# Strassen jobs beside the attention units, and the output projection as one Strassen block product

## The chip, the cores and the metric

One core of a Trainium2 chip. Its engines are TensorE (PE in the profile), VectorE (DVE), ScalarE (ACT), GpSimd (POOL) and SyncE (SP, which only issues transfers here). They run their own instruction streams and meet at semaphores. The metric is the device time of one execution in microseconds.

## The reference

A decoder layer on x of 2 x 512 x 1024 with a context of 2 x 1024 x 1024, in three parts that are each added to x:

```python
q, k, v = ln(x) @ Wq, ln(x) @ Wk, ln(x) @ Wv      # 32 query heads, 8 key/value heads of 128
q, k = rope(q), rope(k)
attn = softmax(causal(q @ k.T / sqrt(128)))       # 4 query heads share a key/value head
x = x + (attn @ v) @ Wo                           # Wo: 4096 x 1024
x = x + fake_quant(ln(x)) @ fake_quant(ctx)       # 8 bit grids
x = x + experts(ln(x))                            # top 16 of 64 low-rank experts
```

## The kernel before

Every float32 product is made of three passes on float32r pairs (`PASSES`): a high part that ScalarE casts (`*_high`) and a low part, the difference, that VectorE or GpSimd makes (`*_low`). TensorE does high by high, high by low, low by high.

**Projections.** `PANELS = 12` panels of 512 output features: K (0, 1), Q (2 to 9), V (10, 11). Each panel is one Strassen (Winograd) block product of the form [features x inner] by [inner x rows], with seven products P1 to P7 on halves; the blocks of x are made once (`fills`, in `xc`). Weight quarters A00, A10, A01, A11 arrive in `wraw`; GpSimd makes the sums S1, S3, S2, S4 in place of the quarters (`weight_sum`), and the low parts (`w_low`, L431). VectorE adds the products up and turns queries and keys (`rope`, L710 to L714). Results go to DRAM (`qk_dram`, `v_dram`).

**Attention units.** 64 units, one for each head and batch; unit u belongs to head group u // 8 and batch (u % 8) // 4. TensorE runs for unit u: `scores(u)` (L1001, 12 matmuls), a piece, `mix(u-1)` (L1029), a piece, `turn_probs(u)` (L1018, 10 transposes). Between, VectorE reads the scores with the mask (`peaks`, L792), ScalarE takes the exponentials (`exps`, L595), VectorE scales (`normalise`, L805), and after the transposes ScalarE and VectorE split the turned probabilities (`probs_high`, `probs_low`). Each query tile is loaded (ring of three), cast by ScalarE (`q_high`, L572) and split by GpSimd (`q_low`, L476) one unit ahead. `mix` is cast and split (`out_high`, `out_low`).

**Pieces.** The output projection is 128 pieces of 12 matmuls (`piece`, L1042) in banks 6 and 7, each of one group's four heads, 128 rows and 512 columns, and VectorE adds each to `resid` (`add_piece`, L821). Units 5 to 63 hold two each; nine come after the last mix. Wo is split by ScalarE and GpSimd in the units (`wo_high`, `wo_low`, L481), and the context is quantised there (`scale_ctx`, `quant_ctx`).

**The order** is written out by hand in every engine's program: five loops over u, with the position of each call fixed. x is loaded a second time into `resid` when the last panel is stored (L402), since the projections work in it. After the pieces VectorE takes the row statistics, and a second block of instructions (`mix_and_experts`, from L1131 on) begins when all engines have ended the first.

```python
for u in range(UNITS):            # TensorE
    scores(u)
    for n in pieces_of(u)[:1]: piece(n)
    if u > 0: mix(u - 1)
    for n in pieces_of(u)[1:]: piece(n)
    turn_probs(u)
```

## Time and profile before

| | us |
|---|---|
| median of three runs | 1380.82 (1379.29 to 1381.46) |
| the profiled execution | 1379.72 |
| its span | 1377.9 |
| TensorE busy in the span | 1319.8 (96%) |
| VectorE, ScalarE, GpSimd busy | 913.1, 610.7, 552.0 |

The span is what the trace covers. Its stages: blocks of x and first products to about 57 us, panels to 505, units from 505 to 1174, the last pieces to 1201, the second block from 1207 on. In a timeline a row gives start, duration, engine, line and operation; "x10" is a run of ten instructions; brackets hold the idle time before it and what ended it. The mean of a matmul counts its whole way through the array, so two overlap: the pitch of starts is what a matmul costs. PEclk is the granted share of TensorE's 2.4 GHz. Spans on POOL are rough.

### The profile page before, as it was taken

The numbers are of one execution on the slowest core, as the hardware profiler recorded it, in microseconds if no ns is written. First come the engines' busy times: TensorE is split into PE (matmuls) and PEld (weight loads), VectorE is DVE, ScalarE is ACT, GpSimd is POOL, SyncE is SP. The second block draws the span as 40 slices with busy tenths as digits, with TensorE's granted clock in tenths as the row PEclk, the third lists the DMA queues.
The fourth block names the chain that finished last, engine by engine and source line by source line (L and its number), as shares of the span: only waits on it lengthen the run. The fifth ranks groups of instructions, "written<-read, shape, count | busy, mean of one in ns | idle before, by whom it ended". The sixth has DMA issues, their size and how long they took to land. (4 is left out here: it accounts for less than half of the span.)

```text
span 1377.9 us, 19834 instructions
## 1 busy us (share of the span) xinstructions
PE 1319.8 (96%) x7217; PEld 1131.7 (82%) x7217; DVE 913.1 (66%) x2108; ACT 610.7 (44%) x1236; POOL 552.0 (40%) x290
## 2 busy tenths in 40 slices
PE   5999999999999986999999999999999999988998
PEld 4778888888889986888888888888888888766887
DVE  7788777777776235666666676576666666678653
ACT  3512222122222236566565565556656565156540
POOL 5676776666676643223142241323313232022000
PEclk9999999999999998999999999999999999999999
DMA  7033333232333156112223222222312210300001
GB/s 259 9 130 123 115 115 114 87 111 89 113 115 123 62 195 211 54 41 90 71 85 92 70 84 62 85 69 70 107 39 84 78 61 1 122 3 16 32 32 46
DMA packets 78432, 119.32 MB, mean 87 GB/s; under 512 B 5744, under 2 KB 42608, under 8 KB 78336
## 3 DMA queue, kind: packets, MB, share of 16 engines
q1 hardware_dynamic: 78336, 118.06, 26.0%
q8 instruction: 58, 0.95, 0.3%
q14 instruction: 38, 0.31, 0.1%
HBM read 88.68 MB, written 29.36 MB: 86 GB/s over the span
## 5 line engine op out<-in xcount | busy, mean ns | idle before, releaser
L977 PE MATMUL banks<-xc,wring 128*128 128x512 f32 x1680 | 385.5, 391 | 5.8 <-DVE banks L748 3.3
L977 PEld LDWEIGHTS banks<-xc,wring 128*128 128x128 f32 x1680 | 316.0, 189 | 72.7 <-issue 6.8
L476 POOL TENSOR_TENSOR q_lo<-q_raw,q_hi 128x512 fp32r<-128x512 f32 x64 | 83.0, 1297 | 452.8 <-ACT q_hi L572 452.8
L431 POOL TENSOR_TENSOR wring<-wraw,wring 128x1024 fp32r<-128x1024 f32 x72 | 172.7, 2399 | 120.2 <-ACT wring L553 120.2
L1042 PE MATMUL banks<-wo_hi,oT_hi 128*128 128x512 f32 x512 | 203.5, 398 | 2.5 <-DVE resid L821 2.5
L1042 PE MATMUL banks<-wo_hi,oT_lo 128*128 128x512 f32 x512 | 200.8, 392 | 0.0
L1042 PE MATMUL banks<-wo_lo,oT_hi 128*128 128x512 f32 x512 | 200.6, 392 | 0.0
L553 ACT CAST wring<-wraw 128x1024 fp32r<-128x1024 f32 x72 | 75.7, 1053 | 273.2 <-PE banks L977 116.3
L595 ACT ACTIVATE prob<-prob,shift 128x512 f32<-128x512 f32 (+3 forms) x256 | 140.9, 552 | 34.6 <-DVE shift L792 33.1
L588 ACT CAST pT_hi<-banks 128x512 fp32r<-128x512 f32 (+1 forms) x192 | 86.6, 524 | 149.6 <-PE banks L1018 149.6
L821 DVE TENSOR_TENSOR resid<-banks,resid 128x512 f32<-128x512 f32 x128 | 87.9, 687 | 88.6 <-PE banks L1042 88.4
L783 DVE TENSOR_TENSOR pT_lo<-banks,pT_hi 128x512 fp32r<-128x512 f32 (+1 forms) x192 | 103.8, 595 | 24.9 <-ACT pT_hi L588 24.9
L1042 PEld LDWEIGHTS banks<-wo_hi,oT_lo 128*128 128x128 f32 x512 | 96.1, 188 | 20.9
L1042 PEld LDWEIGHTS banks<-wo_hi,oT_hi 128*128 128x128 f32 x512 | 96.4, 188 | 19.5 <-issue 2.9
L792 DVE CUSTOM_DVE_ANT_0 prob<-banks,mask 128x512 f32<-128x512 f32 (+3 forms) x256 | 110.1, 485 | 1.3 <-PE banks L1001 0.8
L1042 PEld LDWEIGHTS banks<-wo_lo,oT_hi 128*128 128x128 f32 x512 | 96.4, 188 | 16.3
L1018 PE MATMUL banks<-ident,prob 128*128 128x128 f32 x640 | 82.7, 277 | 16.9 <-DVE oT_lo L810 12.9
L1018 PEld LDWEIGHTS banks<-ident,prob 128*128 128x128 f32 x640 | 74.7, 143 | 26.8 <-DVE prob L805 16.6
L1001 PE MATMUL banks<-kT_hi,q_hi 128*128 128x512 f32 (+3 forms) x256 | 89.3, 349 | 0.0
L1001 PE MATMUL banks<-kT_lo,q_hi 128*128 128x512 f32 (+3 forms) x256 | 84.4, 330 | 0.0
L1001 PE MATMUL banks<-kT_hi,q_lo 128*128 128x512 f32 (+3 forms) x256 | 84.1, 328 | 0.0
L1029 PE MATMUL banks<-pT_hi,v_lo 128*128 128x512 f32 (+3 forms) x256 | 82.8, 323 | 0.0
(169 smaller groups left out, 2369.1 us busy)
## 6 DMA issues: line engine op xcount, KB each, us to landing
qk_dram<-resid SPq DMA_DIRECT2D x80, 256.0 KB, 2.0
wraw<-in_L_attn_Wq SPq DMA_DIRECT2D x32, 512.0 KB, 4.5
q_raw<-qk_dram SPq DMA_DIRECT2D x64, 256.0 KB, 4.0
raw<-in_L_attn_Wo SPq DMA_DIRECT2D x32, 512.0 KB, 4.1
resid<-in_x SPq DMA_DIRECT2D x16, 512.0 KB, 8.0
spare<-in_ctx SPq DMA_DIRECT2D x16, 512.0 KB, 3.7
wraw<-in_L_attn_Wk SPq DMA_DIRECT2D x8, 512.0 KB, 9.5
wraw<-in_L_attn_Wv SPq DMA_DIRECT2D x8, 512.0 KB, 4.4
```

What stands on the lines that cost most here:

```text
L431: nc.gpsimd.tensor_tensor(wring[:, 1, n % 3, :], factor(s, p), as32(wring[:, 0, n % 3, :]), ALU.subtract).then_inc(w_lo, 1)
L476: nc.gpsimd.tensor_tensor(qh[1][:, u % 3, :], q_raw[:, u % 3, :], as32(qh[0][:, u % 3, :]), ALU.subtract).then_inc(q_lo, 1)
L588: nc.scalar.copy(pT[0][:, CHUNKS[c][0]:CHUNKS[c][0] + CHUNK_WIDTH[c]], turned_chunk(turned, mixed, c)).then_inc(pT_hi, 1)
L595: nc.scalar.activation(prob[:, sl], prob[:, sl], ACT.Exp, bias=shift[:, i:i + 1], scale=-1.0, accum_out=total[:, i:i + 1]).then_inc(exp_do ...
L783: nc.vector.tensor_tensor(pT[1][:, sl], turned_chunk(turned, mixed, c), as32(pT[0][:, sl]), ALU.subtract).then_inc(pT_lo, 1)
L792: nc.vector.tensor_tensor_reduce(out=prob[:, PROB_AT[i]:PROB_AT[i] + w], in0=score[:, s, c:c + w], in1=mask[:, H - w:H], scale=-SCALE, sca ...
L821: nc.vector.tensor_tensor(resid[:, t, sl], bank[n % 2][:], resid[:, t, sl], ALU.add).then_inc(added, 1)
L977: ins = nc.tensor.matmul(dst, wring[:, a, n % 3, k * 256 + fb * P:k * 256 + (fb + 1) * P], xc[:, XI[p], c, k, :], start=first, stop=(k == ...
L1001: ins = nc.tensor.matmul(score[:, s, c:c + w], qh[a][:, u % 3, i * P:(i + 1) * P], kT[e][:, h % 2, 0:w], start=(p == 0), stop=(p == 2))
L1018: ins = nc.tensor.transpose(dst[:, col:col + P], prob[:, PROB_AT[i] + j * P:PROB_AT[i] + (j + 1) * P], ident[:])
L1029: ins = nc.tensor.matmul(mixed[:, j * P:H], vv[a][:, h % 2, j, :], pT[c][:, KEYS_AT[j]:KEYS_AT[j] + w], start=(j == 0 and p == 0), stop=(j ...
L1042: ins = nc.tensor.matmul(bank[n % 2], oT[a][:, h % 2, k, t * P:(t + 1) * P], wo[c][:, 2 * half + k // 2, (k % 2) * 512:(k % 2) * 512 + 512 ...
```

## The change

**Projections.** `PANELS` is 5: K (0, 1), the queries of head group 0 (2), V (3, 4). The queries of groups 1 to 7 are 14 narrow panels (`NARROW`) of 256 features, each again a Strassen product of seven; each of its products is one job of 12 matmuls of 512 columns (`job`), 98 in all. `PLACES` puts them in the units: one in unit 1, two in each of units 2 to 33, then two or one, to unit 52, at the places where the pieces were. The order within a narrow panel is `SEQ`. Weights come as four loads of 256 KB for a panel (`load_narrow`), ScalarE casts them (`narrow_high`), GpSimd makes sums and low parts (`narrow_sums`, `narrow_low`), VectorE reads the banks and multiplies by the rope tables (`read_job`), GpSimd adds the two halves (`turn_added`), SyncE stores (`keep_turned`). The last panel's P5 and P3 partly move into units 0 and 1. The rings of queries go from three to two.

**Output projection.** The heads' outputs are stored to DRAM by name (`keep_out`, batch 1 with the sign turned, by `O_STORES` up to four copies of 256 KB a unit), and GpSimd adds blocks of four heads onto the copies with accumulating DRAM to DRAM transfers (`accumulate`, 28 of 1 MB), which gives the sums S1 to S4. The product is then one Strassen product over batch, half of the heads and half of the columns. P1 is in 16 first steps of 12 matmuls (`first_step`, 15 of them in units 56 to 63, with `first_high` and `first_low`). The other six products (`OUT`) are 8 steps of 24 matmuls each (`step`), after the last unit; `step_high` and `step_low` split both operands, `wt` makes Wo's differences on VectorE, `read_banks` and `add_copies` add to `resid`. The second load of x, the quantising of the context, and the load of A_w and B_w move to this stage. Wo's quarters are loaded whole as the memory of the jobs comes free, half of the last one (`w01_b`) after the last mix.

```diff
-PANELS = 12
+PANELS, TURNED = 5, 3
+LASTP = PANELS - 1
...
+SEQ = ("P1", "P6", "P2", "P7", "P5", "P4", "P3")
+NARROW = 14
+JOBS = 7 * NARROW
+PLACES = ([(1, 1)] + [(u, p) for u in range(2, 34) for p in (0, 1)]
+          + [(u, p) for u in range(34, UNITS) for p in (0, 1) if p == 0 or u % 4 != 1])
+JOB_AT = {pl: j for j, pl in enumerate(PLACES[:JOBS])}
...
+OUT = ("P2", "P3", "P6", "P7", "P5", "P4")
+PAIRS = 8
+FIRST_STEPS = 2 * PAIRS
+REST = [(u, p) for u in range(LAST_JOB_UNIT + 2, UNITS) for p in (0, 1)]
+STEP_AT = {pl: n for n, pl in enumerate(REST[len(REST) - FIRST_STEPS + 1:])}
...
         def load_q(u):
-            if u >= 3:
-                sp.wait_ge(q_lo, u - 2)
-            sp.dma_start(q_raw[:, u % 3, :], qk_dram[GROUPS + 4 * (u // 8) + u % 4, (u % 8) // 4]
-                         ).then_inc(q_in[u % 3], 16)
...
+                sp.wait_ge(q_lo, u - 1)
+            if u >= 8:
+                n = turn_needed(u)
+                sp.wait_ge(q_kept[n % 2], 16 * (n // 2 + 1))
...
+        def keep_out(u):
+            sp.wait_ge(o_copied, u + 1)
+            for name in o_names(u):
+                sp.dma_start(o_dram[name][o_place(u)[1]], o_st[u % 2][:]).then_inc(o_kept[u % 2], 16)
...
+        def load_step(s):
+            m, q = s // PAIRS, s % PAIRS
+            if s < 2:
+                sp.wait_ge(fa_lo, FIRST_STEPS - 1 + s)
+            else:
+                sp.wait_ge(oa_lo, s - 1)
+            name = {"P2": "A01", "P3": "S4", "P6": "S2", "P7": "S3", "P5": "S1", "P4": "N11"}[OUT[m]]
...
+            if (s, c) == (LASTP, "C10"):
+                sp.wait_ge(w_lo, len(ORDER))
+                load_narrow(0)
+                load_narrow(1)
+        for u in range(1, UNITS):
+            if u + 2 < UNITS:
+                load_q(u + 2)
+            if u % 4 == 1 and half_of(u) + 1 < HALVES:
+                load_kv(half_of(u) + 1)
+            if (u - 1, 0) in JOB_AT:
...
+                keep_turned(JOB_AT[u - 1, 0])
+            if u >= 2:
+                keep_out(u - 2)
+            for j in jobs_of(u):
+                if j % 7 == 6 and j // 7 + 2 < NARROW:
+                    load_narrow(j // 7 + 2)
+            if (u - 1, 1) in JOB_AT:
+                keep_turned(JOB_AT[u - 1, 1])
...
+        keep_out(UNITS - 2)
+        load_first(FIRST_STEPS - 1)
+        load_step(0)
+        load_step(1)
+        keep_out(UNITS - 1)
+        sp.wait_ge(mix_done, UNITS)
+        load_wo(w01[1], PAIRS, 1, w01_in[1])
         for t in range(TT):
             sp.dma_start(resid[:, t, :], x_t[t]).then_inc(x_in[t], 16)
...
+        load_ctx(0)
+        load_ctx(1)
+        for s in range(2, STEPS):
+            load_step(s)
+            n = s - 4 * PAIRS
+            if 2 <= n < 2 * KT:
+                load_ctx(n)
+            if s == 4 * PAIRS:
+                sp.wait_ge(wt_sum, 4 * PAIRS)
+                sp.dma_start(a_rows[:], A_w.rearrange("(n p) c -> p n c", p=P)).then_inc(rows_in, 16)
+                sp.dma_start(b_rows[:], B_w.rearrange("(n p) c -> p n c", p=P)).then_inc(rows_in, 16)
...
+        def narrow_low(j):
+            pool.wait_ge(n_hi, j + 1)
+            nc.gpsimd.tensor_tensor(n_ring(1, j), n_factor(j), as32(n_ring(0, j)), ALU.subtract).then_inc(n_lo, 1)
...
+        def narrow_sums(j):
+            e, use = j // 7, 16 * (j // 14 + 1)
+            if j % 7 == 1:
+                pool.wait_ge(n_in[e % 2][QUARTER["A10"]], use)
+                pool.wait_ge(n_in[e % 2][QUARTER["A11"]], use)
+                nc.gpsimd.tensor_tensor(n_ta[:], n_quarter(e, "A10"), n_quarter(e, "A11"), ALU.add).then_inc(n_sum, 1)
+                nc.gpsimd.tensor_tensor(n_quarter(e, "A10"), n_quarter(e, "A00"), n_quarter(e, "A10"),
+                                        ALU.subtract).then_inc(n_sum, 1)
+                pool.wait_ge(n_sum, 4 * e + SUMS["S3"])
+                nc.gpsimd.tensor_tensor(n_quarter(e, "A00"), n_ta[:], n_quarter(e, "A00"),
+                                        ALU.subtract).then_inc(n_sum, 1)
+            elif j % 7 == 6:
+                pool.wait_ge(n_in[e % 2][QUARTER["A01"]], use)
+                pool.wait_ge(n_sum, 4 * e + SUMS["S2"])
+                nc.gpsimd.tensor_tensor(n_quarter(e, "A01"), n_quarter(e, "A01"), n_quarter(e, "A00"),
+                                        ALU.subtract).then_inc(n_sum, 1)
...
+        def turn_added(j):
+            if SEQ[j % 7] not in TURNS:
+                return
+            n = 4 * (j // 7) + TURNS[SEQ[j % 7]]
+            pool.wait_ge(job_read, 6 * (j // 7) + j % 7)
...
+            nc.gpsimd.tensor_tensor(q_made[:, n % 2, :], n_turn[:, 0, :], n_turn[:, 1, :], ALU.add
+                                    ).then_inc(turn_made, 1)
+        def accumulate(name, source, g, before):
+            k = 4 * (g % 4)
+            if before:
+                pool.wait_ge(s_added[name], 16 * before)
+            nc.gpsimd.dma_start(out=o_dram[name][k:k + 4].rearrange("k p c -> (k p) c"),
+                                in_=o_dram[source][k:k + 4].rearrange("k p c -> (k p) c"),
+                                accum_op=ALU.add, max_dma_last_dim=8192).then_inc(s_added[name], 16)
...
         for u in range(UNITS):
+            if (u - 1, 0) in JOB_AT:
+                turn_added(JOB_AT[u - 1, 0])
             if u >= 1 and u + 1 < UNITS:
                 q_low(u + 1)
             if u % 4 == 2 and half_of(u) + 1 < HALVES:
                 k_low(half_of(u) + 1)
                 v_low(half_of(u) + 1)
-            for m in wo_after(u):
-                wo_low(m)
+            for j in jobs_of(u + 1):
+                narrow_sums(j)
+                narrow_low(j)
+            if (u - 1, 1) in JOB_AT:
+                turn_added(JOB_AT[u - 1, 1])
+            for f in steps_of(u + 1):
+                first_low(f)
+            if u % 8 == 2 and u >= 8:
+                accumulate_negated(u // 8 - 1)
+            if u % 8 == 6 and u >= 32:
+                accumulate_plain(u // 8)
+        first_low(FIRST_STEPS - 1)
+        accumulate_negated(GROUPS - 1)
...
+        def narrow_high(j):
+            e, p = j // 7, SEQ[j % 7]
...
+            if p in ("P1", "P2", "P4"):
+                act.wait_ge(n_in[e % 2][QUARTER[FACTOR[p]]], 16 * (e // 2 + 1))
+            else:
+                act.wait_ge(n_sum, 4 * e + SUMS[{"P6": "S2", "P7": "S3", "P5": "S1", "P3": "S4"}[p]])
+            nc.scalar.copy(n_ring(0, j), n_factor(j)).then_inc(n_hi, 1)
...
         for u in range(UNITS):
             if u > 0:
                 probs_high(u - 1)
+                if (u - 1, 1) in JOB_AT:
+                    keep_job(JOB_AT[u - 1, 1])
+                if (u - 1, 1) in STEP_AT:
+                    keep_first(STEP_AT[u - 1, 1])
                 if u + 1 < UNITS:
                     q_high(u + 1)
             if u % 4 == 2 and half_of(u) + 1 < HALVES:
                 k_high(half_of(u) + 1)
                 v_high(half_of(u) + 1)
-            for m in wo_after(u):
-                wo_high(m)
+            for j in jobs_of(u + 1):
+                narrow_high(j)
+            if (u + 1, 0) in STEP_AT:
+                first_high(STEP_AT[u + 1, 0])
             exps(u)
             normalise_wide(u)
+            if (u, 0) in JOB_AT:
+                keep_job(JOB_AT[u, 0])
+            if (u, 0) in STEP_AT:
+                keep_first(STEP_AT[u, 0])
+            if (u + 1, 1) in STEP_AT:
+                first_high(STEP_AT[u + 1, 1])
             if u > 0:
-                out_high(u - 1)
-            if u % 4 == 1:
-                scale_ctx(half_of(u))
+                keep_out(u - 1)
         probs_high(UNITS - 1)
-        out_high(UNITS - 1)
+        first_high(FIRST_STEPS - 1)
+        step_high(0)
+        keep_out(UNITS - 1)
+        keep_first(FIRST_STEPS - 1)
+        for s in range(1, STEPS):
+            step_high(s)
...
+        def read_job(j):
+            e, p, b = j // 7, SEQ[j % 7], job_bank(j)
+            if p == "P1":
+                return
...
+                dve.wait_ge(job_read, 6 * e + 3)
+                nc.vector.tensor_tensor(n_u[:, 0, :], b, n_u[:, 0, :], ALU.add)
+                link(nc.vector.tensor_tensor(b, b, n_u[:, 1, :], ALU.add))
+                job_turn(b, 4 * e + TURNS[p])
+            elif p == "P4":
...
+        def step_low(s):
+            m, q = s // PAIRS, s % PAIRS
+            dve.wait_ge(oa_hi, s + 1)
+            nc.vector.tensor_tensor(oa[1][:, s % 2, :, :], oraw[:, s % 2, :, :], as32(oa[0][:, s % 2, :, :]),
+                                    ALU.subtract).then_inc(oa_lo, 1)
+            dve.wait_ge(ob_hi, s + 1)
+            nc.vector.tensor_tensor(ob[1][:, s % 2, :, :], out_factor(m, q), as32(ob[0][:, s % 2, :, :]),
+                                    ALU.subtract).then_inc(ob_lo, 1)
...
+        def read_banks(m):
+            p = OUT[m]
+            dve.wait_ge(step_done, PAIRS * (m + 1))
...
+        for s in range(STEPS):
+            m, q = s // PAIRS, s % PAIRS
+            step_low(s)
+            if m < 4:
+                wt(m, q)
+            else:
+                quant_ctx(s - 4 * PAIRS)
+            if m >= 1 and q == 1:
+                read_banks(m - 1)
+            if m >= 1 and q == 2:
+                add_copies(m - 1)
+            if m == 5 and 3 <= q < 3 + TPB:
+                row_stats(nc, resid, stats, moments, q - 3, link)
+        row_scale_in(nc, moments, lnw, slice(0, TPB), var_ready)
+        quant_rows(0)
+        read_banks(5)
+        add_copies(5)
+        for t in range(TPB, TT):
             row_stats(nc, resid, stats, moments, t, link)
-        row_scale_in(nc, moments, lnw, slice(0, TPB), var_ready)
-        add_piece(PIECES - 8)
-        add_piece(PIECES - 7)
-        quant_rows(0)
-        for n in range(PIECES - 6, PIECES):
-            add_piece(n)
-            if n >= PIECES - 4:
-                dve.wait_ge(added, n + 1)
-                row_stats(nc, resid, stats, moments, n - (PIECES - 4) + TPB, link)
         row_scale_in(nc, moments, lnw, slice(TPB, TT), var_ready)
...
+        def job(j):
+            e, i, p = j // 7, j % 7, SEQ[j % 7]
+            pe.wait_ge(n_lo, j + 1)
...
+            for k in range(KH):
+                for n, (a, c) in enumerate(PASSES):
+                    ins = nc.tensor.matmul(job_bank(j), n_ring(a, j)[:, k * P:(k + 1) * P], xc[:, XI[p], c, k, :],
+                                           start=(opens and k == 0 and n == 0), stop=(k == KH - 1 and n == 2),
+                                           skip_group_check=True)
+            ins.then_inc(job_done, 1)
...
+        def step(s):
+            m, q = s // PAIRS, s % PAIRS
+            pe.wait_ge(oa_lo, s + 1)
+            pe.wait_ge(ob_lo, s + 1)
...
+            for k in range(2):
+                for t in range(TPB):
+                    for i, (a, c) in enumerate(PASSES):
+                        ins = nc.tensor.matmul(step_bank(m, t), oa[a][:, s % 2, k, t * P:(t + 1) * P],
+                                               ob[c][:, s % 2, k, :], start=(q == 0 and k == 0 and i == 0),
+                                               stop=(q == PAIRS - 1 and k == 1 and i == 2), skip_group_check=True)
+            ins.then_inc(step_done, 1)
...
             scores(u)
-            for n in pieces_of(u)[:1]:
-                piece(n)
+            if u == 0:
+                product(LASTP, "P5", (1,))
+                product(LASTP, "P3", (0,))
+            if u == 1:
+                product(LASTP, "P3", (1,))
+            place(u, 0)
             if u > 0:
                 mix(u - 1)
-            for n in pieces_of(u)[1:]:
-                piece(n)
+            place(u, 1)
             turn_probs(u)
-        piece(PIECES - 10)
+        first_step(FIRST_STEPS - 1)
         mix(UNITS - 1)
-        for n in range(PIECES - 9, PIECES):
-            piece(n)
-        pe.wait_ge(masked_done, 4 * UNITS)
+        for s in range(STEPS):
+            step(s)
```

## Rows read from the trace of the kernel before

**Rows 1.** Table of stretches, 700 to 800 us; the header names the columns.
```profile
core 0: us, PE busy (x) PEld busy (x) DVE busy (x) ACT busy (x) POOL busy (x), PEclk, DMA share, GB/s
700.00:800.00 100.00, 99.84 (x552) 86.91 (x551) 64.41 (x188) 60.49 (x147) 30.99 (x20) 1.00 0.27 83
```

**Rows 2.** Timeline of GpSimd: start, us, line, operation; sums of two query panels.
```profile
379.34 2.40 POOL L439 TENSOR_TENSOR ta<-wraw 128x1024 f32<-128x1024 f32 x1
...
417.47 2.41 POOL L439 TENSOR_TENSOR ta<-wraw 128x1024 f32<-128x1024 f32 x1
```

**Rows 3.** Timeline of TensorE over one unit.
```profile
706.65 1.25 PE L1018 MATMUL banks<-ident,prob 128*128 128x128 f32 x10
707.66 0.48 PE L1001 MATMUL banks<-kT_hi,q_hi 128*128 128x512 f32 x1
...
709.67 0.40 PE L1042 MATMUL banks<-wo_hi,oT_hi 128*128 128x512 f32 x1
...
712.44 0.39 PE L1029 MATMUL banks<-pT_hi,v_hi 128*128 128x512 f32 x1
...
714.30 0.45 PE L1042 MATMUL banks<-wo_hi,oT_hi 128*128 128x512 f32 x1
...
717.11 1.25 PE L1018 MATMUL banks<-ident,prob 128*128 128x128 f32 x10
```

**Rows 4.** Timeline of ScalarE over the same unit.
```profile
708.51 0.65 ACT L572 CAST q_hi<-q_raw 128x512 fp32r<-128x512 f32 x1
...
710.16 0.73 ACT L595 ACTIVATE prob<-prob,shift 128x512 f32<-128x512 f32 x1
```

**Rows 5.** Timeline of GpSimd in the same unit.
```profile
709.23 1.30 POOL L476 TENSOR_TENSOR q_lo<-q_raw,q_hi 128x512 fp32r<-128x512 f32 x1 [6.78 <-ACT q_hi L572]
```

**Rows 6.** Timeline of VectorE in the same unit.
```profile
712.71 0.88 DVE L805 TENSOR_SCALAR prob<-prob,inv 128x384 f32<-128x384 f32 x3
```

**Rows 7.** Waits of TensorE: waited for, us in total, times, longest.
```profile
PE banks L1018 <- DVE oT_lo L810: 12.9, 10, 5.8
PE banks L1018 <- DVE prob L805: 4.0, 1, 4.0
...
PE banks L1042 <- DVE resid L821: 2.5, 1, 2.5
```

**Rows 8.** Table of stretches in the first units.
```profile
511.40:515.90 4.50, 4.46 (x22) 4.22 (x23) 2.46 (x6) 3.04 (x6) 1.00 (x1) 0.65 0.95 349
521.00:526.50 5.50, 5.50 (x27) 5.06 (x25) 4.01 (x12) 2.62 (x6) 1.60 (x2) 0.69 1.06 378
532.40:540.30 7.90, 7.86 (x34) 7.31 (x34) 4.12 (x14) 5.83 (x14) 3.63 (x2) 0.62 0.45 160
549.50:552.00 2.50, 2.44 (x18) 2.35 (x18) 1.16 (x2) 1.78 (x4) 0.00 (x0) 1.00 0.00 0
```

**Rows 9.** Groups by line: line, operation, busy us, mean ns, idle before.
```profile
L710 DVE TENSOR_TENSOR resid<-banks,sin 64x512 f32<-64x512 f32 x80 | 55.4, 693 | 3.6 <-PE banks L977 1.3
```

**Rows 10.** DMA issues of the page: count, KB, median us to landing.
```profile
q_raw<-qk_dram SPq DMA_DIRECT2D x64, 256.0 KB, 4.0
```

**Rows 11.** Timeline of TensorE, two units without a piece.
```profile
541.77 1.28 PE L1018 MATMUL banks<-ident,prob 128*128 128x128 f32 x10 [1.49 <-DVE oT_lo L810]
...
549.56 1.28 PE L1018 MATMUL banks<-ident,prob 128*128 128x128 f32 x10 [2.62 <-DVE oT_lo L810]
```

**Rows 12.** DMA view of 506 to 527 us.
```profile
DMA packets 3058, 7.07 MB, mean 337 GB/s; under 512 B 247, under 2 KB 1027, under 8 KB 3056
```

**Rows 13.** Timeline of ScalarE in that stretch.
```profile
523.90 0.62 ACT L572 CAST q_hi<-q_raw 128x512 fp32r<-128x512 f32 x1 [1.92 <-DMA q_raw<-qk_dram]
```

**Rows 14.** Timeline at the end of attention, VectorE.
```profile
1201.48 0.69 DVE L821 TENSOR_TENSOR resid<-banks,resid 128x512 f32<-128x512 f32 x1 [0.46 <-PE banks L1042]
...
1203.77 0.17 DVE L168 TENSOR_SCALAR lnw<-moments 128x4 f32<-128x4 f32 x1
...
1206.88 0.69 DVE L1351 TENSOR_SCALAR raw<-raw 128x1024 f32<-128x1024 f32 x1 [0.96 <-PEq L116]
```

More of the change, by code:

```diff
@@ L124, in build @@
[L124 to L126 removed]
+            with ExitStack() as sems:
+                attention(nc, hold(sems), sems, x_t, Wq, Wk, Wv, Wo, cos_in, sin_in, (x1s, x1z, x2s, x2z),
+                          ctx_in.rearrange("b k n -> (b k) n"), qk_dram, v_dram, o_dram, A_w, B_w, proj, heads,
+                          narrow, outp, *shared)
             mix_and_experts(nc, hold(es), es, out_t, Wr, keys, *shared)
```

674 lines of the change are left out of this document (464 added, 210 removed).

## The prediction

> **What bounds the kernel now.** I read the table of stretches first, then a timeline of one attention unit on each engine, then the waits, and the chain of waits last, which covers only the final stages. In a stretch of attention TensorE is busy 99.8 of 100 us at a granted clock of 1.00 (2.4 GHz), VectorE 64, ScalarE 60, GpSimd 31 [rows 1]: TensorE sets the time. The panels of projections are as full: one panel of queries takes 38.13 us for 168 matmuls of 512 columns, 0.227 us each [rows 2]. A unit takes 10.46 us: transposes 1.01, scores 2.01, a piece 2.77, mix 1.86, a piece 2.81 [rows 3]. That is 4.88 of attention and 2.79 for each of two fillers of 12 matmuls.
>
> Inside that period the other engines run one chain. Counted from the start of the transposes (706.65), ScalarE ends the high part of the next queries at 2.5 and starts the exponentials at 3.5 [rows 4]; GpSimd ends the low part of those queries at 3.9 [rows 5]; VectorE ends the last scaled probabilities at 6.9, which is 3.4 after the exponentials began [rows 6]. TensorE asks for them at 10.46. So the exponentials may begin 3.5 us late before TensorE waits. That slack is what the change lives on.
>
> **What the matmuls give.** Projections have the same matmuls before and after: 5 panels, and 98 jobs of 12 in place of 7 panels of 168. The output projection had 128 pieces of 12 (1536); it gets 16 first steps of 12 and 48 steps of 24 (1344). 192 fewer x 0.227 = **-43.6 us**, all on TensorE. The waits of TensorE in the first units (12.9 + 4.0) and for one piece bank after the last unit (2.5) go too, since the units 1 to 4 get fillers: **-19.4** [rows 7]. With them goes slow clock: 4.5 x 0.35 + 5.5 x 0.31 + 7.9 x 0.38 = **-6.3** [rows 8]. By this alone the span would be 1377.9 - 69.3 = 1308.6.
>
> **What the jobs add beside the units.** VectorE gets 18 operations for 7 jobs at 0.7 us [rows 9] instead of three for a unit, 3.6 us a unit against 2.1: busy about 79%, behind exponentials and matmuls, costed at nothing (without that cover 1.5 us a unit, 80 us). SyncE issues up to 13 transfers in a unit, and the query load has a ring of two in place of three; I cost it at nothing while a load takes the 4.0 us of the median [rows 10], and return to it as a rival.
>
> The cost that I do see is an order. In iteration u ScalarE runs `narrow_high` for the jobs of u+1 before `exps(u)`. For P6 it waits for S2, the third of three sums that GpSimd makes in `narrow_sums` of the same iteration, behind `q_low(u+1)`, which itself waits for ScalarE. Queued behind the waiting ScalarE instruction are the exponentials, and TensorE's transposes wait for those. A 512-column operation of GpSimd takes 1.30 [rows 5].
> - P6 in the second place: 3.9 (queries) + 1.3 (low of P1) + 3.9 (sums) = 9.1; high part 0.6; exponentials at 9.7, probabilities at 13.1 instead of 10.46: 2.7 us of wait.
> - P6 in the first place: the unit before had S4 ahead of P3, so its exponentials start at about 6.2, its probabilities end at 9.6, and VectorE's five operations of P5 end at 13.2, which is 2.8 in the new unit. `turn_added` 1.3, queries 1.3, sums 3.9 = 9.3; two high parts 1.2; + 3.4 = 14.0: 3.5 us of wait, or 2.9 where one place follows.
>
> `PLACES` puts P6 second in units 5, 12, 19, 26, 33 (5 x 2.7 = 13.5), first in 9, 16, 23, 30 (14.0) and in 37, 41, 45, 49 (4 x 2.9 = 11.6). Where keys and values are split in the same iteration GpSimd has 2.6 more: P6 of 19 and 23 (5.2), and P3 of units 11 and 15 (2.6 and 1.9). Together **+49**. A wait of 2.6 is followed by a clock of 1.00 here, one of 4.0 by 0.65 [rows 7, 8, 11]; so only the two longest pay for the clock, 1.5 each: **+3**. Its bounds are 0 and 15 x 3.0, the loss of the longest slow stretch.
>
> The start: the first weights are loaded after the last P4's tile, job 1 needs three sums, and query 2 is loaded behind 2 MB. Between 0 and 5.8 + 3.0 (the worst of the old start [rows 7, 8]), taken at **+2.8**. Units 53 to 55 have no filler: a unit without one took 549.56 - 541.77 = 7.8 [rows 11], less the removed VectorE step 7.1, against 4.88 of work: 3 x 2.2 = **+6.6**.
>
> **What the block product adds.** The last first step waits for high and low parts that start only after the last probabilities are copied, at 1.9 where now the query's cast begins [rows 4]: 0.6 on ScalarE, then GpSimd's 1.3 for 512 elements and about twice that for 1024, to 6.3, where TensorE is free at 1.0. **+5.3**, and 2 of clock. A step is 24 x 0.227 = 5.45 us; ScalarE needs at most four times 0.65 [rows 4] for it, 2.6, VectorE two subtractions and a weight difference of about 1.2 each (an estimate: 0.69 for 512 elements plus as much again less the start), 3.7. So steps are bound by TensorE, except where P5's four bank reads, the quantising of the context and the statistics meet: **+3**.
>
> The **restart** is the second large cost. After the last mix SyncE queues half of a Wo quarter (2 MB), all of x (4 MB), two context tiles (1 MB), and only then the load for step 2. The trace has this burst: 7.07 MB took 21 us at 337 GB/s, and a query load issued in it held ScalarE up [rows 12, 13]. 7.75 MB take 23 us; 11.8 + 23 = 34.3 after the last transposes, + 3.4 for high and low = 37.7, where steps 0 and 1 end at 21.8: 16 us. The last three accumulating transfers (3 MB, read twice and written once) run at the same time on the same engines. No row shows such a transfer; at nothing they leave 16, at twice their bytes and this rate they make it 33. I take **+20**, nearer the lower end since the row of 337 GB/s already had other traffic, and 3 for the clock. The Trainium skill ("DMA: Bandwidth & Descriptors", Anatomy of one DMA) gives a GpSimd-issued transfer about 2.0 us plus its bytes at 436 GB/s; by it, as an estimate, three of 1 MB would add some 7 us and this term would be 23. No run so far shows it.
>
> Loading A_w and B_w (4 MB) ahead of step 33's load delays it past its slack by **+4.3** (4.5 MB at 337 GB/s are 13.4 us, slack about 9). The tail: now 5.4 us lie between VectorE's read of the last piece and the next block, of which 1.6 are one tile's statistics and 3.1 the scales [rows 14]. Then it will be two bank reads and two additions of 1024 elements (5.1), four tiles' statistics (6.4) and 3.1, together 14.6: **+9.2**, and 1.4 for a clock that has fallen.
>
> **The sum.** 1308.6 + 2.8 + 49 + 3 + 6.6 + 7.3 + 23 + 3 + 4.3 + 10.6 = 1418.2 us of span. The profiled execution took 1379.72 with a span of 1377.9, so 1.8 more: **1420 us**. It was 1.1 below the median of 1380.82, which I leave aside.
>
> **Rivals.**
> - *The sums are not late* (faster). If GpSimd had S2 before ScalarE asks, the 49 + 3 vanish: 1368. For it: GpSimd is idle two thirds of the time [rows 1]. Against: it must run `q_low` first, which waits for ScalarE until 2.5.
> - *The restart is hidden as well*: also without the 23: 1345. For it: nothing but that the loads of steps 0 and 1 are ahead.
> - *Transfers are late in the units* (slower still). Stores of the signed sums (1 MB in a unit), weights (1 MB) and 3 MB of accumulation meet once per group of heads, and a late query load stops the exponentials as it did at 523.9. At 5.8 of wait + 3.0 of clock seven times: +62, 1482. It decides from a load of over about 8 us instead of 4; before, seen only in the burst.
> - The forecast itself is slower; the mechanism on the faster side decides at 3.5 us of lateness.
>
> **How the numbers follow.** Forecast 0.50; sums not late 0.16; restart hidden too 0.12; late transfers 0.12; in between, with part of the 49, 0.10, of which 0.05 lie below the old time, 0.04 at it and 0.01 above. The change does what it says in every case, since the counts follow from the loops. Faster by over 0.2% (about what a measurement can tell from no change): 0.16 + 0.12 + 0.05 = 0.33; within it 0.04; slower 0.50 + 0.12 + 0.01 = 0.63. The range reaches from the second rival to 30 above the forecast, which takes in the bounds of the restart and half of the clock's: 1348 to 1452. The forecast's own range is 1395 to 1450.
>
> **What would show it.** In the changed profile: ScalarE waiting for GpSimd's sum before `n_ring` of P6, some 13 times, and TensorE before the transposes in the same units, 2.5 to 3.5 us each (5 to 6 in two); a jobs unit without P6 still at 10.5; one gap of 15 to 33 us before the third step; steps of 5.45 us; about 14.5 us from the last step to the next block. No waits of ScalarE for GpSimd would make the first rival right; waits for `q_raw` the third. Wrong from the start would be a step bound by VectorE: at 6 us a step the product would cost 26 more.

## The result and the profile after

The changed kernel takes **1514.34 us** (median of 4 runs, 1510.90 to 1518.62), the kernel before 1381.11 beside it (1379.29 to 1381.46): a ratio of 1.0969, 95% interval 1.0939 to 1.0999. The forecast was 1420 with a range of 1348 to 1452. The direction was right, the size was not: the change costs 133 us, not 39.

The head of the page of the kernel after, with its two lines in 40 slices that moved most:

```profile
span 1508.9 us, 19933 instructions
PE 1302.0 (86%) x7025; PEld 1111.5 (74%) x7025; DVE 947.6 (63%) x2024; ACT 698.9 (46%) x1385; POOL 638.3 (42%) x451
...
PE   5999999998998898999999628682899989968998
...
PEclk9999999999999999999999869987899999999999
...
q0 software_dynamic: 4032, 29.36, 9.9%
```

TensorE was busy 96% of the span before. Now it is 86%, with the loss at slices 23 to 28, some 830 to 1060 us: the end of the attention units and the restart. The last line is a queue that the kernel before hardly used: 29.36 MB of accumulating transfers.

What ended the waits of the kernel after (engine, line waited at, releaser: us in total, times, longest):

```profile
PE banks L1457 <- DVE prob L1175: 51.7, 20, 7.6
ACT nring_hi_a L860 <- POOL nraw L697: 50.9, 8, 7.5
...
PE banks L1457 <- ACT o_st L925: 47.2, 12, 27.4
...
PE banks L1529 <- DVE ob_lo L1184: 39.6, 4, 31.4
ACT oa_hi L892 <- DMA oraw<-o_A: 35.3, 1, 35.3
ACT q_hi L846 <- DMA q_raw<-qk_dram: 34.4, 4, 25.1
ACT nring_hi_b L860 <- POOL nraw L697: 32.2, 5, 6.7
...
PE banks L1487 <- DVE n_turn L1113: 11.2, 17, 1.0
```

L1457 are the transposes of a unit, L1529 the 48 steps, L1487 the jobs. Against 19.4 us before [rows 7], TensorE now waits 98.9 before transposes and 39.6 before steps.

The table lays the forecast's sum beside TensorE's timeline, cut at the transposes of three units, at the last step's last matmul (row at 1323.49) and at the next block's first row (1337.57):

| stretch | forecast | after | difference |
|---|---|---|---|
| start to unit 1 | 251.2 | 251.4 | +0.2 |
| unit 1 to 51 (jobs) | 563.8 | 577.4 | +13.6 |
| unit 51 to 63 | 109.9 | 175.9 | **+66.0** |
| unit 63 to the last step (last first step, restart, 48 steps) | 306.3 | 318.8 | +12.5 |
| tail | 16.0 | 14.1 | -1.9 |
| rest | 171.0 | 171.3 | +0.3 |

The sum is 90.7 us. Nearly three quarters of it lie in twelve units, for which the sum had 6.6 us beyond their work. Below, a period is the time from one unit's transposes to the next unit's. TensorE's timeline there (start, us, line, operation, idle time before it and its releaser):

```profile
853.15 2.37 PE L1457 MATMUL banks<-ident,prob 128*128 128x128 f32 x10 [7.63 <-DVE prob L1175]
...
893.73 2.37 PE L1457 MATMUL banks<-ident,prob 128*128 128x128 f32 x10 [27.43 <-ACT o_st L925]
...
918.50 1.28 PE L1457 MATMUL banks<-ident,prob 128*128 128x128 f32 x10 [2.30 <-ACT o_st L925]
...
1010.96 0.77 PE L1503 MATMUL banks<-ob_hi,oa_hi 128*128 128x512 f32 x1 [5.04 <-POOL ob_lo L748]
1060.88 0.77 PE L1529 MATMUL banks<-ob_hi,oa_hi 128*128 128x512 f32 x1 [31.41 <-DVE ob_lo L1184]
```

The releaser named at 893.73 is only the last of a row. ScalarE's and SyncE's timelines show what stood ahead of it:

```profile
888.21 0.62 ACT L846 CAST q_hi<-q_raw 128x512 fp32r<-128x512 f32 x1 [25.05 <-DMA q_raw<-qk_dram]
```

```profile
851.75 18.65 SPq L499 DMA_DIRECT2D w<-in_L_attn_Wo  x8
870.44 5.62 SPq L499 DMA_DIRECT2D w_a<-in_L_attn_Wo  x2
876.16 2.60 SPq L467 DMA_DIRECT2D q_raw<-qk_dram  x1
```

SyncE issues ten transfers of 1 MB of output weights in unit 53, and only then the next query load. The DMA view of 838 to 895 us says how long that is:

```profile
DMA packets 9874, 18.71 MB, mean 328 GB/s; under 512 B 472, under 2 KB 1540, under 8 KB 9743
```

The long periods behind it (11.9 to 19.3 us in units 56 to 62, where the forecast has 10.46) have another cause, an order on ScalarE:

```profile
916.29 0.62 ACT L875 CAST oa_hi<-oraw 128x512 fp32r<-128x512 f32 x1 [0.26 <-PE banks L1503]
916.82 1.04 ACT L877 CAST ob_hi<-w 128x1024 fp32r<-128x1024 f32 x1
917.76 0.59 ACT L925 ACTIVATE o_st<-banks 128x512 f32<-128x512 f32 x1
```

The high copies of a first step wait until the step just done has left its ring place (first row), and the copy of the unit's output stands behind them. That copy frees the bank into which TensorE transposes at 918.50.

Part of the time is clock. In the stretch of those twelve units the granted clock is 0.85 (columns as in [rows 1]):

```profile
829.00:1005.00 176.00, 116.55 (x604) 101.45 (x603) 64.45 (x203) 89.10 (x203) 81.13 (x53) 0.85 0.61 190
```

### The profile page after: what moved, and what is told of

Its sections match the earlier page's. It is cut to its first block and busy times, and to the rows that moved or that the text cites. A ratio compares the mean times of both kernels' runs of the same rounds, so it can differ in the third digit from the quotient of the medians.

```text
span 1508.9 us, 19933 instructions
## 1 busy us (share of the span) xinstructions
PE 1302.0 (86%) x7025; PEld 1111.5 (74%) x7025; DVE 947.6 (63%) x2024; ACT 698.9 (46%) x1385; POOL 638.3 (42%) x451
## 3 DMA queue, kind: packets, MB, share of 16 engines
q0 software_dynamic: 4032, 29.36, 9.9%
## 5 line engine op out<-in xcount | busy, mean ns | idle before, releaser
L1529 PE MATMUL banks<-ob_hi,oa_hi 128*128 128x512 f32 x384 | 151.3, 394 | 39.6 <-DVE ob_lo L1184 39.6
L1457 PE MATMUL banks<-ident,prob 128*128 128x128 f32 x640 | 90.1, 293 | 99.1 <-DVE prob L1175 51.7
L1457 PEld LDWEIGHTS banks<-ident,prob 128*128 128x128 f32 x640 | 77.6, 150 | 115.1 <-DVE prob L1175 63.7
L1529 PE MATMUL banks<-ob_lo,oa_hi 128*128 128x512 f32 x384 | 150.8, 393 | 0.0
L1529 PE MATMUL banks<-ob_hi,oa_lo 128*128 128x512 f32 x384 | 150.6, 392 | 0.0
L913 ACT ACTIVATE prob<-prob,small 128x512 f32<-128x512 f32 (+3 forms) x256 | 140.8, 553 | 11.8 <-DVE small L1162 11.7
L1487 PE MATMUL banks<-xc,nring_hi_a 128*128 128x512 f32 x400 | 125.2, 394 | 5.0 <-DVE n_turn L1113 5.0
L1487 PE MATMUL banks<-xc,nring_hi_b 128*128 128x512 f32 x384 | 120.6, 395 | 6.2 <-DVE n_turn L1113 6.2
L1418 PE MATMUL banks<-xc,wring 128*128 128x512 f32 x504 | 119.2, 397 | 5.7 <-DVE banks L1085 3.3
L1418 PEld LDWEIGHTS banks<-xc,wring 128*128 128x128 f32 x504 | 95.8, 192 | 26.5 <-issue 6.7
L1529 PEld LDWEIGHTS banks<-ob_hi,oa_hi 128*128 128x128 f32 x384 | 73.1, 190 | 56.4 <-issue 41.2
L636 POOL TENSOR_TENSOR wring<-wraw,wring 128x1024 fp32r<-128x1024 f32 x30 | 71.9, 2399 | 58.6 <-ACT wring L827 58.6
## 6 DMA issues: line engine op xcount, KB each, us to landing
o_S<-o_S POOLq DMA_DIRECT2D x12, 1024.0 KB, 14.1
w<-in_L_attn_Wo SPq DMA_DIRECT2D x12, 1024.0 KB, 17.8
```

Of the source, the lines that this page charges most:

```text
L636: nc.gpsimd.tensor_tensor(wring[:, 1, n % 3, :], factor(s, p), as32(wring[:, 0, n % 3, :]), ALU.subtract).then_inc(w_lo, 1)
L913: nc.scalar.activation(prob[:, sl], prob[:, sl], ACT.Exp, bias=shift[:, i:i + 1], scale=-1.0, accum_out=total[:, i:i + 1]).then_inc(exp_do ...
L1418: ins = nc.tensor.matmul(dst, wring[:, a, n % 3, k * 256 + fb * P:k * 256 + (fb + 1) * P], xc[:, XI[p], c, k, :], start=first, stop=(k == ...
L1457: ins = nc.tensor.transpose(dst[:, col:col + P], prob[:, PROB_AT[i] + j * P:PROB_AT[i] + (j + 1) * P], ident[:])
L1487: ins = nc.tensor.matmul(job_bank(j), n_ring(a, j)[:, k * P:(k + 1) * P], xc[:, XI[p], c, k, :], start=(opens and k == 0 and n == 0), stop ...
L1529: ins = nc.tensor.matmul(step_bank(m, t), oa[a][:, s % 2, k, t * P:(t + 1) * P], ob[c][:, s % 2, k, :], start=(q == 0 and k == 0 and i == ...
```

## The experiments

All are measured beside the kernel before; differences are between medians. The theory is that the 133 us are independent losses (counted from the old kernel; from the sum's 1308.6 of matmuls, with the 1.8 outside the span, they are 204): GpSimd's sums (A), the weights ahead of the query loads (B), the order of the output's copy (C), the restart (D). The first four kernels undo one each.

**A: GpSimd's sums earlier.** `narrow_sums` makes P6's first two sums as part 0, its third as part 1 and P3's as part 2.

```diff
+        narrow_sums(0, 0)
         for u in range(UNITS):
...
             for j in jobs_of(u + 1):
-                narrow_sums(j)
                 narrow_low(j)
+                if j % 7 == 0:
+                    narrow_sums(j, 1)
+                elif j % 7 == 2:
+                    narrow_sums(j, 2)
+                elif j % 7 == 6 and j + 1 < JOBS:
+                    narrow_sums(j + 1, 0)
```

> Only the order of GpSimd's weight sums in the narrow jobs is changed: the two first sums of P6 follow the low copy of the previous column's last job, the third follows the low copy of P1, that of P3 follows the low copy of P2. Theory A (the exponentials of a unit stand on ScalarE behind a high copy that waits for these sums): the 14 long periods of 12.3 to 16.8 us fall to 10.5 to 11, GpSimd's sums no longer end a wait of ScalarE's ring copies, and the time falls from 1514 by 45 to 62 us, to 1452 to 1469. Rival: GpSimd is simply late in these units (key and value copies, the additions of the turned queries), so that the order of its work moves the wait to another place; then the time falls by less than 20 us, to above 1494.

1471.47 us (1470.76 to 1473.65): **42.9 us less**, 2 short of the range. ScalarE's waits for `nraw` fall from 127.7 us in 27 waits to these 21.5 in 5, and TensorE's wait for the probabilities falls with them:

```profile
ACT nring_hi_a L871 <- POOL nraw L701: 12.1, 3, 5.0
ACT nring_hi_b L871 <- POOL nraw L701: 9.4, 2, 5.9
...
PE banks L1468 <- DVE prob L1186: 20.7, 10, 8.6
```

The last was 51.7 in 20 waits. The mechanism holds, its size a little less than expected. What stays are units with a late chain of their own: in units 11 and 18 (periods of 13.0 and 13.2) ScalarE still waits 5.9 and 5.0 us for the third sum, which GpSimd reaches late behind the splits of keys and values (in unit 11 three accumulates to issue as well), and in unit 28 (13.2) the output's copy waits 6.1 us until its buffer has been stored.

**B: the weights in pieces**, each behind the unit's query load.

```diff
-                load_wo(w00, 0, 0, w00_in)
...
-                load_wo(w10, 2 * PAIRS, 0, w10_in)
-                load_wo(w11, 2 * PAIRS, 1, w11_in)
-                load_wo(w01[0], 0, 1, w01_in[0])
+            for n in WO_AT.get(u, ()):
+                load_piece(n)
```

> Only the issue of the output weights' first 14 MB on SyncE's queue is changed: one piece of 1 MB in each of units 51 to 62, two in 53 and 54, each behind the query load of its unit, instead of 4 MB in unit 51 and 10 MB in unit 53. Theory B (the query loads queue behind the weights, 18.71 MB at 328 GB/s): the periods of units 53 and 55 fall from 14.3 and 32.6 to about 11, ScalarE's waits of 7.8 and 25.1 us for q_raw go, and the time falls by 33 to 40 us, to 1474 to 1481. Rival (the loads would be as late through the transfers of the units themselves, stores and accumulates): a fall of less than 12 us, to above 1502, with the waits for q_raw moved to units 56 to 62.

1490.81 (1489.48 to 1495.34): **23.5 less**, not 33 to 40. Of the 34.4 us of waits for `q_raw` 1.1 are left, but 8.6 us before unit 55's transposes stay and unit 60 has become longer (period 23.1). ScalarE's timeline names another transfer in both places:

```profile
865.65 0.62 ACT L888 CAST oa_hi<-oraw 128x512 fp32r<-128x512 f32 x1 [5.15 <-DMA oraw<-o_A]
...
930.64 0.62 ACT L888 CAST oa_hi<-oraw 128x512 fp32r<-128x512 f32 x1 [8.01 <-DMA oraw<-o_A]
```

The second waits beside an accumulate. The DMA view of 918 to 944 us, 40 slices:

```profile
DMA  9999999999999996999999624910000000000000
GB/s 214 217 232 228 232 219 228 228 222 230 230 216 230 217 192 207 381 373 402 399 406 406 246 85 145 331 44 0 0 0 0 0 0 0 0 0 0 0 0 2
```

For ten microseconds all 16 engines are busy and move 220 GB/s; then the accumulates end and the same engines move 400. That is a fifth loss (E), which I had not separated.

**C: the output's copy first.**

```diff
+            if u > 0:
+                keep_out(u - 1)
             if (u + 1, 1) in STEP_AT:
                 first_high(STEP_AT[u + 1, 1])
-            if u > 0:
-                keep_out(u - 1)
```

> Only the order of two things on ScalarE is changed: the copy of the unit's output (o_st) goes ahead of the high copies of the first step of the next unit's second place. Theory C (the transposes of a unit wait for the copy of the output, which stands behind a copy that waits for the step just done): the waits of TensorE for the o_st copy in units 56 to 62, 47 us in 12 waits now, fall to below 12, and the time falls by 14 to 20 us, to 1494 to 1500; the three longest waits, with the accumulates about them, may stay. Rival: the output's copy is late for its own sake (the mix and the store of o_st two units earlier, slowed by the accumulates), so the wait stays over 35 us and the time within 5 us of 1514.

1500.64 (1497.48 to 1504.37): **13.7 less**. The ordinary first-step unit falls from 12.9 to 11.1 us and no wait for `o_st` is left among the large ones; the 26 us of unit 55 are put down to `prob` instead, which is the same query load by another releaser. The mechanism holds and the size is just short of its 14 to 20, with units 58 and 60 still long (15.3 and 17.9).

**D: the restart**, with what steps 2 to 11 don't need behind their loads.

```diff
-        load_wo(w01[1], PAIRS, 1, w01_in[1])
-        for t in range(TT):
-            sp.dma_start(resid[:, t, :], x_t[t]).then_inc(x_in[t], 16)
-        load_ctx(0)
-        load_ctx(1)
         for s in range(2, STEPS):
             load_step(s)
...
+            if 4 <= s < 4 + TT:
+                sp.dma_start(resid[:, s - 4, :], x_t[s - 4]).then_inc(x_in[s - 4], 16)
...
```

> Only SyncE's order after the last unit is changed: the last 2 MB of the output weights go in two pieces behind the loads of steps 2 and 3, the eight residual tiles behind the loads of steps 4 to 11, the first two context tiles behind that of step 14. Theory D1 (step 2's load stands in the queue behind 8 MB): the idle time before step 2 falls from 31.4 to 3 to 8 us and the time by 23 to 28 us, to 1486 to 1491. Theory D2 (the accumulates of the last group hold the DMA engines in that stretch): the idle time stays at 15 to 20 us and the time falls by 11 to 16 us, to 1498 to 1503.

1493.76 (1492.70 to 1495.33): **20.6 less**, where D1 had 23 to 28 and D2 11 to 16. The idle time of 31.41 before step 2 is gone; what TensorE still waits there is 2.95 before step 3 and 4.09 before step 4:

```profile
1040.45 0.77 PE L1536 MATMUL banks<-ob_hi,oa_hi 128*128 128x512 f32 x1 [2.95 <-DVE ob_lo L1191]
...
1053.05 0.55 PE L1536 MATMUL banks<-ob_hi,oa_hi 128*128 128x512 f32 x1 [4.09 <-DVE ob_lo L1191]
```

So D1 names what step 2 waited for, and part of it came back behind: TensorE's waits before steps are 15.3 in all, from 39.6.

**Together, and without the accumulates.**

> The four edits (sums earlier, weights in pieces, order of the output's copy, order after the last unit) together. Each alone took from 1514.3: 42.8, 23.5, 13.7 and 20.5 us, in all 100.5. If they are independent losses, as the theory has it, the time is 1414 (1408 to 1420). If they share a cause (one wait uncovers another), the sum is not reached and the time stays above 1425.

1420.56 (1416.88 to 1422.63), **93.8 less** where the four alone add up to 100.7. They are nearly independent, though the time is 0.6 above the expected range. That this is the number forecast is chance; it says only how much was overlooked.

> The changed kernel without any of its 28 accumulating transfers (the combinations of the attention outputs are not added up in memory, so the output is another). Theory E (these transfers, while they run, hold all DMA engines at some 220 GB/s where 400 go otherwise, and so lengthen the first-step units and the restart): the idle time before step 2 falls from 31.4 to 18 to 22 us, the long periods of units 59 to 61 fall to the 12.9 of their neighbours, 9 us in all, nothing changes before unit 52, and the time falls by 18 to 24 us, to 1490 to 1496. Rival (the accumulates only run in time that nobody needs): within 5 us of 1514.

1477.77 (1476.20 to 1482.24): **36.6 less**, half as much again as theory E allowed. By the timeline 17.8 of it lie between units 51 and 63 and 15.4 in the restart, where the idle time is

```profile
1026.73 0.76 PE L1525 MATMUL banks<-ob_hi,oa_hi 128*128 128x512 f32 x1 [16.01 <-DVE ob_lo L1180]
```

Theory E had the wrong units: 13.2 of the 17.8 us lie in units 53 to 55, where an accumulate meets the burst of weights (their periods fall from 14.3, 8.0 and 32.6 to 8.4, 7.1 and 26.2). Units 59 to 61, where E expected 9 us, fall by 2.9 in all, and unit 60 still takes 18.1.

The DMA views of the two restarts, first the kernel after (1014 to 1060), then without accumulates (997 to 1027):

```profile
GB/s 0 0 0 0 0 235 212 360 378 399 390 281 201 239 265 224 285 217 278 224 292 224 289 203 281 228 310 406 417 431 417 413 427 399 408 388 387 157 7 0
...
q0 software_dynamic: 432, 3.15, 32.8%
...
o_S<-o_N POOLq DMA_DIRECT2D x3, 1024.0 KB, 17.7
```

```profile
GB/s 0 0 0 0 0 112 251 175 344 377 410 380 412 407 423 407 393 426 404 393 426 426 382 421 426 393 404 426 393 410 421 385 388 388 390 142 0 0 0 60
```

Three accumulates of 1 MB took 32.8% of 46 us on all engines, 15.1 us, or 209 GB/s. That is about the 15.4 us by which the idle time differs.

> The four edits, and none of the 28 accumulating transfers (the output is another). It prices these transfers where the four losses are gone. Theory E: the first-step units fall to periods of about 10.5 to 11, the restart's idle time to under 3 us, and the time is 1385 to 1395, some 20 to 28 us below the four edits. Rival: the loads in pieces are what collides with the query loads, with or without the accumulates: less than 8 us below the four edits.

1386.01 (1385.29 to 1386.76), 34.6 below the four edits: more than expected, and about the price that the accumulates have beside the other losses. No idle time is left before steps 2 to 4, but units 58 and 60 stay at 15.3 and 16.0, so their length isn't the accumulates' either.

**The accumulates of the last group moved**, alone in the changed kernel:

```diff
-        accumulate_negated(GROUPS - 1)
+        one_negated(GROUPS - 1, 0)
+        pool.wait_ge(step_done, 10)
+        one_negated(GROUPS - 1, 1)
+        pool.wait_ge(step_done, 18)
+        one_negated(GROUPS - 1, 2)
```

> The changed kernel with one edit: of the last group's three accumulates only that into S4, which the second product reads, follows the last unit; that into S2 waits for step 10 and that into S1 for step 18. Without all accumulates the idle time before step 2 was 16.0 instead of 31.4 us. Theory G (the restart pays for the bytes of the accumulates that run in it): with one of the three left it is 20 to 23 us, and the time falls by 8 to 11 us, to 1503 to 1506. Rival (the plain accumulate of unit 62 and the first one already fill the stretch in which step 2's load waits): below 4 us.

1502.32 (1499.91 to 1502.72): **12.0 less**, one more than expected, and the idle time before step 2 is 21.53. With three accumulates in the restart it is 31.4, with one 21.5, with none 16.0: about 5 us for each.

**The search for a version that gains.** Five more kernels and one of them without accumulates build on the four edits; their edits are told in the expectations.

> The four edits, with each unit's weight piece behind the first-step loads instead of ahead of them, and three more: the adapters' weights in eight pieces from step 34 on instead of two transfers ahead of step 33's load; the copies of P1 added to the last quarter of the rows during P7's successor, and half of the last four tiles' statistics taken ahead of the last read; the three accumulates of groups 5 and 6 one a unit instead of three in a row. Expected against the four edits: 8 us from the adapters' weights (waits of 8.2 us in the step stage), 5 from the tail (2.49 of additions and 4 x 0.69 of statistics), 5 to 10 from the first-step units: 1390 to 1397. Rival: the VectorE's own time in the last steps is the limit, and the tail keeps its length.

1398.38 (1397.53 to 1400.36), 22.2 below the four edits and 1 above the expected range. The wait of 7.2 us for the adapters' weights is gone, and the tail's last wait is `PEq` 3.6 where it was 8.5.

> The eight edits of the run before, and three in the attention units: ScalarE's and GpSimd's work on the next half's values goes one unit behind that on its keys; the last first step's high copies go ahead of the last unit's probabilities (and its load ahead of a store); the copies of the first eight first steps' banks go ahead of unit 60's exponentials. Expected from the trace of the run before: 5 us from the last first step (idle 6.2 before it), 3 to 5 from unit 60 (period 15.97), 4 from unit 58 (period 15.28, idle 4.66), 3 to 6 from the long periods of units 11 to 28: 1398 less 15 to 20, 1378 to 1384, level with the kernel before. Rival: ScalarE is full in these units whatever the order (the work is only handed to the next unit), and the time stays above 1390.

1383.73 (1383.27 to 1387.40), 14.7 less again; ratio to before 1.0029 (1.0017 to 1.0041). ScalarE was late by its order, not full: unit 60 falls to 12.0 and unit 58 to 11.2.

> As the run beside it, but the accumulating transfers take each head's output from SBUF (112 of 256 KB, three or one for a head, issued by GpSimd in every unit) instead of 28 of 1 MB from memory to memory; the data read again from memory fall by 29 MB. Theory F1 (an accumulating transfer costs DMA time by the bytes that it adds, wherever these come from): the same time as the run beside it within 4 us, with the transfers spread over the units but two of the last ones still in the restart. Theory F2 (the reading back is a third of the load): 4 to 10 us faster. Rival: 84 more issues of some 0.85 us on GpSimd make its low copies late: over 5 us slower.

1398.03 (1397.10 to 1399.22): 14.3 **slower** than the run beside it. The rival is right in its sign alone. TensorE waits 33.4 us in 12 waits for the output's copy, and ScalarE makes that copy late because the buffer is still being read:

```profile
ACT o_st L951 <- DMA o_S<-o_st: 34.3, 15, 5.8
```

```profile
833.36 2.62 POOL L757 DMA_DIRECT2D o_S<-o_st  x3
...
844.21 0.60 ACT L951 ACTIVATE o_st<-banks 128x512 f32<-128x512 f32 x1 [5.81 <-DMA o_S<-o_st]
```

So the delay comes from the held buffer and not from low copies. GpSimd's order has a part in it: unit 53's copy was made at 818.14, its three additions were issued at 833.36 only, and unit 55's copy could start when they had landed. How much is the late issue and how much the transfer, no run separates. F1 and F2 both fail, since the DMA time of the same bytes has grown. The lines of that queue, first of e_eleven (span 1381.9), then of e_direct (span 1395.3):

```profile
q0 software_dynamic: 4032, 29.36, 10.9%
```

```profile
q0 software_dynamic: 16128, 29.37, 13.4%
```

151 us against 187, for four times as many packets. (The transfers also run at other times than those of e_eleven, so the 14.3 are not all due to the source.)

> The eleven edits and two more: the first 4 MB of the output weights in units 51 and 52, two pieces each, so that units 53 and 54 carry one piece of the next instead of two; and VectorE's sums on the last 2 MB of the output weights in steps 6 and 7 instead of 4 to 7. The trace of the eleven edits has ScalarE waiting 7.45 us for q_raw in unit 55 (TensorE idle 7.42) and TensorE idle 2.02 and 7.03 before steps 4 and 5. If both go: 1383.7 less 12 to 16, 1368 to 1372, faster than the kernel before by 0.6 to 0.9 %. Rival: the plain accumulate of unit 54 (at 230 GB/s for 10 us) makes the query load late whatever stands ahead of it, and the last accumulates do so in the restart: above 1379.

1383.06 (1381.51 to 1385.51): no gain; its rival is right. The idle time moved to units 54 and 57 (5.4, and a period of 12.8) and stayed in the restart. There ScalarE waits for step loads issued beside three accumulates:

```profile
944.50 1.05 ACT L937 CAST oa_hi<-oraw 128x1024 fp32r<-128x1024 f32 x1 [7.79 <-DMA oraw<-o_A]
...
956.54 1.04 ACT L937 CAST oa_hi<-oraw 128x1024 fp32r<-128x1024 f32 x1 [10.04 <-DMA oraw<-o_A]
```

> The same without any of the 28 accumulating transfers (the output is another). It gives what they still cost once the other losses are gone: by the theory that most of their price lay in the queueing that the other edits have taken away, less than 6 us below the run beside it; if they cost the 34 us that they cost the four edits, 1340.

1361.73 (1359.81 to 1364.72), 21.3 below the run beside it. So the accumulates keep 21.3 of their 34.6 us with more of the queueing gone; the theory in that expectation (less than 6) is wrong.

> The thirteen edits and three more: the same late accumulates into S2 and S1; no weight piece in unit 54, where an accumulate of 1 MB runs (the pieces of w11, which the second product reads, come last); the second half of the residual rows behind the loads of steps 16 to 19. By the trace of the thirteen edits 2.6 and 6.3 us of idle time before steps 3 and 4 and 5.4 us in unit 54 should go: 1383 less 9 to 14, 1369 to 1374, faster than the kernel before by 0.5 to 0.9 %. Rival: the idle time moves to the next transfer as it did with the last two edits, and the time stays above 1379.

**1373.49 us** (1372.62 to 1373.77), ratio to the kernel before 0.9951 (0.9938 to 0.9963): 0.5% faster than the kernel before, and within the expected 1369 to 1374. Its waits:

```profile
PE banks L1523 <- DVE prob L1226: 26.5, 21, 7.1
PE banks L1449 <- DVE resid L1079: 18.2, 2, 13.6
PE banks L1553 <- DVE n_turn L1164: 13.0, 23, 1.1
PE banks L2058 <- PEq L192: 3.6, 1, 3.6
```

Before the steps 1.4 us in two waits are left. The wait in unit 54, which was to go, is 7.1 us where it was 5.4; in its surroundings (795 to 822 us) three query loads take 11.6 us in the median, beside two accumulates and three weight pieces.

## Why the prediction was wrong, point by point

- **Matmuls, start** (1308.6 and +2.8). Right: unit 1's transposes start 0.2 us from the forecast. TensorE's busy time in e_sixteen, at a clock of 0.990, is 1280.3 against 1319.8.
- **The sums** (+49 and 3). The mechanism is right and so are most sizes: the periods ahead of P6 are 13.15 (second place), 14.37 (first place) and 13.25 (first place, one place following), which is 2.7, 3.9 and 2.8 above 10.46 where 2.7, 3.5 and 2.9 were worked out; the two longest have 5.2 and 6.4 for 5.2. The fifteen long periods lie 48.9 above 10.46 in all; so close a sum is partly luck, since unit 15 has 4.5 for 3.5 and unit 29 has 2.6 for 3.5. The stretch still took 13.6 more than forecast, because "VectorE at nothing" was wrong: a job after P6's place waits until VectorE has read its bank (`n_turn`, 11.2 us in 17 waits), so the period after a long one is 11.5 to 12 in six of nine cases, not 10.46. Undoing the order of the sums gave 42.9 back.
- **"SyncE issues up to 13 transfers in a unit; I cost it at nothing"**. This is the step that failed. I counted transfers and took a median duration, and never added up the bytes that `load_wo` puts in front of one query load: 10 MB, by the 337 GB/s of [rows 12] 31 us. Measured, ScalarE waited 25.05 us for that load, the period of unit 55 was 32.6 us, and B gave 23.5 back. The price of it stood in a row that I used for another term, and [rows 13] even showed the victim. The rival "transfers are late" has the mechanism, but placed it seven times in the group meetings and not once in this burst.
- **First-step units at 10.46.** I took a filler for a filler. A job's high copy waits for a job four places back, a first step's for the one just done; the order on ScalarE was not followed through for units 56 to 62, as it was for the jobs. The periods of units 56 to 62 lie 25.7 above it, and C gave back 13.7.
- **Last first step** (+5.3 and 2). 5.04 of wait measured: right.
- **The restart** (+20, bounds 16 and 33). The bounds held and the choice between them was wrong: 16.0 without accumulates, 31.4 with them. I took a value nearer the lower end for a resource that no row showed; the upper end, twice the bytes, was the physical argument. The rule of the Trainium skill ("DMA: Bandwidth & Descriptors", Anatomy of one DMA) made three accumulates about 7 us, an estimate; here they cost 15.4, so the measurement decides against applying that rule to an accumulating transfer.
- **Accumulates in the units**: nothing in the sum either; 17.8 us in the changed kernel.
- **Steps** (+3 and 4.3): 39.6 - 31.4 = 8.2 in three waits. Right in the sum; the parts are 6.8 for 4.3 (step 33) and 1.4 for 3.
- **The clock** (3, 2, 3 and 1.4 in the sum): too small. The same 7025 matmuls were busy for 1302.0 us at a granted clock of 0.956 over the span, and for 1280.3 at 0.990 in e_sixteen. These 22 us are inside the stretches of the table, and the low clock lies where the waits that the sum left out are (0.85 over 829 to 1005 us).
- **The tail** (14.6 us and 1.4): 13.65 from the read at 1323.92 to the block at 1337.57. Right.
- **The range** reached 32 us above the forecast. It took in the bounds of costs that were in the sum, and nothing for a cost set at zero.

Of the 133 us, the four undone orders account for 94 and the accumulates for 35 more; the four edits without accumulates come within 5.8 us of the kernel before. They are still 76 us above the 1310.4 that the matmuls alone would give, and e_sixteen is 63 above it: the other terms of the sum and waits that no single run here prices.

## What to carry to other kernels

Add up bytes per queue, not transfers: before a term for a queue is set to nothing, take the longest run of bytes ahead of a load that someone waits for, and divide it by the bandwidth of a burst in the trace. A filler with fewer matmuls is not the same filler; follow each engine's order once around the loop for every kind of iteration, and find for each copy what it waits for. Sums made by accumulating transfers took DMA time at half the rate of a load. The 43.6 us saved on TensorE here were worth 6.6 at best, after sixteen edits, and 19.3 with thirteen edits and no accumulates at all (and another output), so those transfers are not the whole reason.

## What the runs showed of the hardware

While accumulating transfers from memory to memory ran in the restart, all 16 DMA engines were busy and moved 200 to 290 GB/s in all, where 380 to 430 went without them: 3.15 MB took 15.1 us of all engines. Taken from SBUF in 256 KB instead, with four times the packets, the same 29.4 MB took 187 us of them in place of 151. The granted clock fell once more where TensorE had waited long (0.85 over 829 to 1005 us, with the waits of 7.63 and 27.43), and with these waits gone it is 0.990 over the span in e_sixteen.
